# Second attention: the products of a pair of heads issued in turn instead of head by head

## What is computed

```python
c_kv = _lin(hidden_states, W_DKV_w, W_DKV_b)
k = _lin(c_kv, W_UK_w, W_UK_b).reshape(b, s, H, D)
v = _lin(c_kv, W_UV_w, W_UV_b).reshape(b, s, H, D)
c_q = _lin(hidden_states, W_DQ_w, W_DQ_b)
q = _lin(c_q, W_UQ_w, W_UQ_b).reshape(b, s, H, D)
scores = jnp.einsum('bqhd,bkhd->bhqk', q, k) * scale
probs = jax.nn.softmax(scores, axis=-1)
attn = jnp.einsum('bhqk,bkhd->bqhd', probs, v).reshape(b, s, H * D)
output = _lin(attn, W_O_w, W_O_b)
```

## Time and profile before

| | |
|---|---|
| median of 3 runs | 826.01 us (824.09 to 826.27) |
| profiled execution, its own time | 827.4 us |
| span of its instructions | 825.6 us |
| mean granted TensorE clock | 0.946 |
| TensorE matmul busy | 741.5 us, 90% of the span, 4504 instructions |
| VectorE, ScalarE, GpSimd busy | 473.3, 322.4, 245.0 us |
| second attention, first to last score product | 364.0 to 551.3 us |

### The profile page before, as it was taken

The page is one execution under the profiler, slowest core; times in us unless marked ns, Lnnn a source line. Parts: engine busy times, 40 slices in busy tenths (PEclk is TensorE's granted clock), DMA queues, the critical chain, the costliest instruction groups (busy, mean ns, idle before and its releaser), DMA issues.

```text
span 825.6 us, 11928 instructions
## 1 busy us (share of the span) xinstructions
PE 741.5 (90%) x4504; PEld 599.1 (73%) x4504; DVE 473.3 (57%) x1058; ACT 322.4 (39%) x771; POOL 245.0 (30%) x328
## 2 busy tenths in 40 slices
PE   4985599999886999797999998987999999999997
PEld 2764378788775888586778776765787777777775
DVE  4789768675448675656553545465344444454544
ACT  2423244544532333244664665572332222222221
POOL 1236411100325522407242333244132222233300
PEclk9988799999998899797998999899899999999999
DMA  6323000000202200001000000002011111111001
GB/s 208 96 65 96 11 1 2 1 2 1 64 20 57 58 2 21 20 20 39 1 1 1 2 2 1 2 1 58 18 39 44 52 39 39 39 39 39 1 1 52
DMA packets 11674, 25.84 MB, mean 31 GB/s; under 512 B 1344, under 2 KB 3392, under 8 KB 11584
## 3 DMA queue, kind: packets, MB, share of 16 engines
q1 hardware_dynamic: 11616, 25.07, 10.6%
HBM read 24.02 MB, written 1.05 MB: 30 GB/s over the span
## 4 chain that ended last, share of the span: by engine, by line
PE 71%; DVE 15%; ACT 5%; issue 5%; POOL 3%; DMA 1%; SPq 0%; DVEq 0%; POOLq 0%; ACTq 0%
PE ps L554 48%; PE ps L649 4%; PE ps L620 4%; PE ps L831 3%; PE ps L632 3%; PE ps L690 2%; ACT AO L1094 2%; PE ps L820 2%; PE ps L562 2%; DVE NB L1161 1%; PE ps L623 1%; PE ps L576 1%; DMA wr<-in_w 1%; PE ps L571 1%; PE ps L580 1%
## 5 line engine op out<-in xcount | busy, mean ns | idle before, releaser
L1685 POOL TENSOR_SCALAR PB<-PB,sml 128x256 f32<-128x256 f32 x128 | 59.2, 482 | 110.7 <-DVE sml L1519 110.7
L1357 DVE TENSOR_TENSOR U<-U,ps 128x512 f32<-128x512 f32 x50 | 34.4, 688 | 83.1 <-PE ps L554 83.1
L1017 ACT CAST VVh<-U 128x512 fp32r<-128x512 f32 x50 | 31.0, 621 | 123.4 <-DVE U L1364 109.0
L554 PE MATMUL ps<-ATh,wh 128*128 128x512 f32 x176 | 72.4, 411 | 4.7 <-POOL wl L1656 2.5
L554 PE MATMUL ps<-ATl,wh 128*128 128x512 f32 x176 | 71.1, 404 | 0.0
L554 PE MATMUL ps<-ATh,wl 128*128 128x512 f32 x176 | 70.9, 403 | 0.0
L1654 POOL TENSOR_SCALAR wh<-wr 128x768 fp32r<-128x768 f32 (+3 forms) x31 | 24.0, 773 | 148.7 <-PE ps L554 148.7
L1369 DVE TENSOR_TENSOR VVl<-U,VVh 128x512 fp32r<-128x512 f32 x50 | 45.7, 914 | 37.2 <-ACT VVh L1017 37.2
L1094 ACT COPY AO<-ps 128x512 f32<-128x512 f32 x64 | 34.8, 589 | 76.0 <-PE ps L820 76.0
L1082 ACT ACTIVATE PB<-ps,sml 128x256 f32<-128x256 f32 x128 | 59.6, 496 | 4.5 <-DVE sml L1513 4.5
L649 PEld LDWEIGHTS ps<-VK,PT 128*128 128x128 f32 x384 | 49.3, 191 | 12.0 <-issue 11.4
(11 more groups left out here) (255 smaller groups left out, 2153.7 us busy)
## 6 DMA issues: line engine op xcount, KB each, us to landing
wr<-in_w SPq DMA_DIRECT2D x32, 384.0 KB, 3.1
wr<-in_w SPq DMA_DIRECT2D x16, 321.0 KB, 3.0
wr<-in_w SPq DMA_DIRECT2D x11, 256.0 KB, 2.7
XO<-in_x SPq DMA_DIRECT2D x2, 512.0 KB, 4.7
out_dram<-XO SPq DMA_DIRECT2D x8, 128.0 KB, 1.8
wr<-in_w SPq DMA_DIRECT2D x2, 416.0 KB, 6.3
AO<-in_sm SPq DMA_DIRECT2D x1, 448.0 KB, 7.4
SELf<-in_sel SPq DMA_DIRECT2D x1, 352.0 KB, 4.2
```

What stands on the lines that cost most here:

```text
L554: t = x.matmul(o, a, b, start=first and i == 0 and c == 0, stop=last and i == n - 1 and c == 2, skip_group_check=skip)
L1017: x.copy((VV if run == "moe" else HH)[c][0][:, :], b[:, :]).then_inc(*mark("hi", "h", run, j, half))
L1357: x.tensor_tensor(b[:, :], a[:, :], bank("u", run, j, half)[:, :], ALU.mult).then_inc(*vacates("u", run, j, half))
L1685: t = x.tensor_scalar(p[:, c, :], p[:, c, :], m[:, 16 + c:17 + c], 1.0, ALU.mult, ALU.mult)
```

## The change

In `l1score` the loop over the two heads moves inside: both banks are taken first, and then head 0 and head 1 get each of the six products in turn. `mm3` is written out for that, so these products now have line L812. In `l1weigh` the two heads alternate over the two halves of the keys; both copies are waited for first, and only one signal is left, after the last product. The copy of the transposes (L1094) waits for that one with both heads.

```diff
             e.wait_ge(*vacated("lq", b, j // 2))
-            for i2 in range(2):
-                o = 64 * i2
-                bk = fills(ring["S"], "ls", i, i2)
-                for qt in range(2):
-                    qs = slice(qt * 128, qt * 128 + 128)
-                    p = mm3(bk[:, qt * 256:qt * 256 + 256], [((qh[o:o + 64, j, qs], ql[o:o + 64, j, qs]),
-                            (CD[0][o:o + 64, b * 256:b * 256 + 256], CD[1][o:o + 64, b * 256:b * 256 + 256]))])
-                p.then_inc(*filled("ls", i, i2))
+            bs = slice(b * 256, b * 256 + 256)
+            bk = [fills(ring["S"], "ls", i, i2) for i2 in range(2)]
+            for qt in range(2):
+                qs = slice(qt * 128, qt * 128 + 128)
+                for c, (l, r) in enumerate(((qh, CD[0]), (qh, CD[1]), (ql, CD[0]))):
+                    for i2 in range(2):
+                        o = slice(64 * i2, 64 * i2 + 64)
+                        p = x.matmul(bk[i2][:, qt * 256:qt * 256 + 256], l[o, j, qs], r[o, bs], start=c == 0, stop=c == 2)
+                        if qt == 1 and c == 2:
+                            p.then_inc(*filled("ls", i, i2))
...
             for i2 in range(2):
                 e.wait_ge(*vacated("lt", i, i2))
-                for kc in range(2):
+            for kc in range(2):
+                for i2 in range(2):
                     p = x.matmul(bk[64 * i2:64 * i2 + 64, 0:256], CN[:, 2 * b + kc, :],
                                  PN[(2 * i + i2) % 4][:, kc * 256:kc * 256 + 256], start=kc == 0, stop=kc == 1)
-                p.then_inc(*(filled("lw", i) if i2 else mark("lw0", i)))
+            p.then_inc(*filled("lw", i))
...
                 if i >= 2:
-                    e.wait_ge(*(have("lw", i - 2) if i2 else at("lw0", i - 2)))
+                    e.wait_ge(*have("lw", i - 2))
```

## The result

The changed kernel takes 816.13 us (median of four runs, 813.39 to 818.43) against 826.14 us of the kernel before (four runs, 824.09 to 827.28). The ratio is 0.988, with a 95% interval of 0.9844 to 0.9917, so 7 to 13 us less. The forecast was 819.8 us, with a range of 816.2 to 823.4.

The account below looks back on a forecast made before the run. TensorE held 71% of the chain of waits, so shorter score blocks count only where it runs through them. 6.3 - 0.05, say 6.2 us, off the 826.01 us median gave 819.8 us, range 816.2 to 823.4.

Parts of the forecast that it names:

- the lag: In each score block of the second attention, head 1 starts 0.35 us behind head 0; the change cuts this to 0.01.
- low-clock stretches: Stretches at granted clock 0.5, holding iterations 11 and 26: 0.59 us gain each; one stretch more or fewer moves 2.4 us.
- the sum: Over the second attention: 15 x 0.34 + 2 x 0.59 = 6.3 us, less 0.05 for the weighing, say 6.2 us gained.
- The price of a block: Each score block gets 0.34 us shorter at full clock, 0.59 us at the low clock.
- The feed limit: Rival in the score blocks: TensorE can't start 12 products at 0.06 us apiece; half gain 822.9 us, none 826.0; chance 0.09.
- In order: Rival in the score blocks: heads really run one behind the other, so the gain is 11.7 us, 814.3 us; chance 0.02.
- The 17 iterations: Iterations 4 to 15, 20, 21, 23, 24, 26, where the chain of waits includes the score block; only these gain.
- The next wait: In iteration 9, the tightest, VectorE's bias is ready 0.40 us before ScalarE uses it, room for 0.34; costed at nothing.
- Weighing and signals: The weighing's new order wins nothing and costs 0 to 0.07 us in the drain, taken as 0.05; signals cost 0.
- The clock rival: Rival in iterations 16 to 19, 25, 27 to 31: TensorE idling lowers the clock, 2.4 us per stretch, 829.4 us; chance 0.05.
- the share of 78%: TensorE's busy share expected at 536.34 to 555.50 us after the change, down from 86%; no full-clock row vouched for it.
- the one-bank wait: In iterations without a projection, the weighing waits for its one bank, so the score block's 0.34 us gains nothing.

Follow-up runs that it names:

- ahead: The changed kernel with one to six products of head 0 issued first in each score block, then the heads in turn; 820.48 us, a single run.
- the repetition: The changed kernel run once more with nothing altered; 817.05 us, ratio 0.9889 to the kernel before.
- scores_only: The changed kernel with the weighing and its signals put back as before, only the scores issued product by product; 817.85 us, ratio 0.9892.
- on_chain: The kernel before with the new score block only in iterations 4 to 15, 20, 21, 23, 24 and 26, old weighing; 814.92 us, ratio 0.9867.

## Why the prediction was right, and where it wasn't

The mechanism was right: the lag, its price, and the iterations in which it counts. The size was not: about a third of the gain came from low-clock stretches that went or got shorter, and the sum took them as they were before. So most of the distance from 819.8 us to the measured median is that one term.

- *The price of a block.* Forecast 1.04 to 0.70 us from first to last start, and 0.59 us at the low clock. Measured 0.70; at the low clock 1.24 for 1.84, 0.60. The feed limit is refuted: 12 products start in 0.70 us, 0.06 apiece.
- *In order.* The in-order rival would have taken 0.69 us a block and 11.7 us in all. The kernel before did have the overlap: the look-ahead kernel shows it coming in steps with what stands ahead. The program-order rule of the Trainium skill's page "TensorE: Matmul & The Clock Gate" (Part 3) doesn't hold here between products on different halves of the rows; in the rows of `ahead`, the sixth product of the program starts with the second (both at 462.83). The measurement decides.
- *Where it counts.* The 17 iterations were right as far as the traces tell them apart: those on the chain at full clock up to 21 got 0.35 to 0.38 us shorter, 16 to 19 and 27 to 30 by no more than 0.02, iterations 0 to 3 together 0.1. Iterations 22 to 25, where the edges of the low-clock stretches moved too, gave 0.65 for the 0.68 of 23 and 24. Two kernels with either half confirmed it, 814.92 and 826.59 us.
- *The next wait.* The room of 0.40 us in iteration 9 held, barely: the iteration went from 5.97 to 5.61 us. The changed kernel's VectorE ends the bias at 414.91 + 0.16 = 415.07, and ScalarE takes it at 415.11, 0.04 us later; the sum had left 0.06.
- *Weighing and signals.* Nothing in the loop, 0.05 and at worst 0.07 in the drain; measured nothing and about 0.1.
- *The mis-sized term.* The low-clock stretches. I counted iteration 26 as 0.59 us and let the clock stretches only widen the range, by one of 2.4 us. It gave 3.26. Iterations 10 and 11 gave 0.5 us where the sum had 0.93; their stretch now begins 1.9 us ahead of the score block (427.89, the block at 429.78) instead of 0.1. That this is the reason was not tested. The stage behind began with one shorter stretch, 0.6 us. Together: 6.3 + 2.7 - 0.4 + 0.6 = 9.2 us, and 0.3 spread over the rest, against 10.0 measured (9.1 in the repetition). I treated the stretches as noise between runs. Inside this stage they weren't: in the four profiles with the new score block in all iterations of the chain (`scores_only`, `on_chain` and the changed kernel twice) they begin at the same distance from the stage's first score product within 0.2 us. One profile of the kernel before couldn't show that.
- *The clock rival.* It didn't come: more idle time in 15 iterations brought no stretch, and the share of 78% that I had worked out for TensorE there was 82% in the changed kernel (525.00 to 543.40 us), at full clock.

## What to carry to other kernels

Two products on different halves of the array's rows run side by side when they stand close in the program; a block of more than four weight-load and product pairs of one half ahead of the other delays that by what is beyond four. Products on different halves of the columns, the weighing's, did so with four ahead; more was not tried. Issue such pairs in turn, and then look whether the block is in the chain of waits: 15 of 32 shortened blocks were worth nothing, and eight of these (16 to 19 and 27 to 30) gave 0.35 to 0.38 us each once the one-bank wait behind them was taken away. A shift of a few microseconds can also take a low-clock stretch away or bring it back, and that was worth as much as eight of the blocks; profile the stage again after each change.

## What was not expected of the hardware

- In `ahead`, head 1's first product started at most 0.01, 0.22 to 0.23 or 0.35 us behind head 0's, by whether one to four, five or six products of head 0 stood ahead of it.
- Iteration 26 took 3.7, 5.2 to 5.6 or 6.9 to 7.1 us by the time at which it came, with the same products behind the same 24 narrow ones. In full stretches TensorE got through 34 products in 6.83 us at a granted clock of 0.50, 1.2 GHz; in the next 6.83 us at 1.00, 2.4 GHz, through 52.
- TensorE, busy 15.02 of 18.40 us in the changed kernel, kept the full clock.
